# A four-stage sequence kernel on one core: the Mamba stage by channel halves, with the orders of all engines planned anew

## The reference, cut to what matters

```python
proj = h @ in_W + in_b
x1, g = (proj[..., :D], proj[..., D:])
xc = conv_general_dilated(xt, conv_w[:, None, :], padding=[(K - 1, 0)], ...)
x1 = silu(transpose(xc + conv_b[:, None]))
dbc = x1 @ dbc_W + dbc_b
delta, Bm, Cm = (dbc[..., :DTR], dbc[..., DTR:DTR + N], dbc[..., DTR + N:])
delta = softplus(delta @ dup_W + dup_b)
A_disc = exp(delta[..., None] * A)
B_x = delta[..., None] * Bm[:, :, None, :] * x1[..., None]
# scan over time: h = a * h + b
y = einsum('tbdn,btn->btd', hs, Cm)
y = silu(g) * y
```

## Time and profile before

| | us |
|---|---|
| median of 3 runs | 870.79 |
| lowest, highest | 868.19, 875.68 |
| the profiled execution | 866.0 |
| its span | 864.2 |
| TensorE busy in it | 695.4 |
| VectorE busy | 634.2 |
| ScalarE busy | 426.1 |
| GpSimd busy | 358.3 |

### The profile page before, as it was taken

One profiled execution on the slowest core, in us unless ns is written; L12 is line 12 of the kernel. 1 busy time (PEld: TensorE's weight loads), 2 busy tenths in 40 slices (PEclk: granted clock), 3 DMA queues, 4 the chain that ended last, 5 costly groups with the idle time before them and its releaser, 6 DMA issues.

```text
span 864.2 us, 12658 instructions
## 1 busy us (share of the span) xinstructions
PE 695.4 (80%) x4232; PEld 414.3 (48%) x4232; DVE 634.2 (73%) x1223; ACT 426.1 (49%) x896; POOL 358.3 (41%) x392
## 2 busy tenths in 40 slices
PE   6479648898789878988899778988798878975777
PEld 2345425445544555555545554456454554443324
DVE  1962575887889786978698687978698768846493
ACT  1325333754477255825474346825483337532542
POOL 6640331753258223942184324922293006400470
PEclk7578978998989998998999788999999698987899
DMA  5231210530145004320243014400432004100320
GB/s 131 85 127 38 82 36 10 184 129 1 38 138 174 16 1 149 131 82 0 71 152 140 0 38 135 157 27 1 135 126 98 2 16 151 47 2 6 122 75 7
DMA packets 40457, 66.11 MB, mean 77 GB/s; under 512 B 7281, under 2 KB 29634, under 8 KB 38082
## 3 DMA queue, kind: packets, MB, share of 16 engines
q1 hardware_dynamic: 38242, 64.57, 22.8%
q10 hardware_dynamic: 2176, 1.05, 0.4%
HBM read 57.68 MB, written 7.86 MB: 76 GB/s over the span
## 4 chain that ended last, share of the span: by engine, by line
PE 45%; DVE 31%; issue 11%; ACT 8%; POOL 2%; DMA 2%; SPq 1%; DVEq 0%; ACTq 0%; POOLq 0%
PE ps_s L1210 13%; PE ps_y L1210 10%; PE ps_f L1210 9%; PE ps_v L1210 8%; DVE shared L1171 5%; DVE mx L1070 4%; PE ps_n L1210 4%; DVE shared L1176 2%; DVE bn L982 1%; ACT ps_f L914 1%; ACT probs L831 1%; DVE z L1115 1%; DVE fmem L963 1%; DVE qamax L952 1%; DVE x L994 1%
## 5 line engine op out<-in xcount | busy, mean ns | idle before, releaser
L739 POOL TENSOR_TENSOR shared<-u,bcrow 128x512 f32<-128x512 f32 x128 | 205.3, 1634 | 107.7 <-DVE u L1160 84.9
L1171 DVE TENSOR_TENSOR_SCAN shared<-ps_f,shared 128x512 f32<-128x512 f32 x128 | 150.6, 1208 | 20.7 <-PE ps_y L1210 7.3
L1070 DVE TENSOR_REDUCE mx<-ps_s 128x2 f32<-128x512 f32 (+1 forms) x192 | 127.5, 687 | 48.8 <-PE ps_s L1210 47.0
L1210 PE MATMUL ps_s<-stack_mem 72*128 72x128 bf16 (+3 forms) x1024 | 149.0, 266 | 10.2 <-ACT probs L831 4.6
L1210 PE MATMUL ps_y<-shared,ident 128*128 128x512 f32 x256 | 122.3, 609 | 14.6 <-DVE shared L1176 14.6
L914 ACT ACTIVATE ps_f<-delta,amat 128x255 f32<-128x255 f32 x256 | 110.1, 476 | 32.7 <-DVE shared L1171 18.9
L1210 PEld LDWEIGHTS ps_s<-stack_mem 74*128 74x128 bf16 (+1 forms) x1024 | 87.2, 106 | 72.0 <-issue 22.2
L831 ACT ACTIVATE probs<-ps_s 128x512 f32<-128x512 f32 x192 | 106.3, 596 | 30.4 <-PE ps_s L1210 30.0
L1210 PE MATMUL ps_y<-zero_bf 128*128 128x512 bf16 x293 | 92.5, 430 | 1.4 <-DVE zero_bf L1007 1.0
L1176 DVE TENSOR_TENSOR shared<-shared,bcrow 128x1024 f32<-128x1024 f32 x64 | 91.2, 1426 | 2.2
L1210 PEld LDWEIGHTS ps_y<-shared,ident 128*128 128x128 f32 x256 | 45.7, 192 | 59.9 <-issue 36.9
(11 more groups left out here) (219 smaller groups left out, 1060.3 us busy)
## 6 DMA issues: line engine op xcount, KB each, us to landing
bcrow<-bc_dram SPq DMA_DIRECT2D x64, 512.0 KB, 4.2
stack_mem<-stack_dram SPq DMA_DIRECT2D x96, 192.0 KB
stack_dram<-parts SPq DMA_DIRECT2D x24, 256.0 KB, 2.3
x_tm<-in_L_attn_x_dram ACTq DMA_DIRECT2D x8, 128.0 KB, 2.2
xb<-in_L_attn_x_dram SPq DMA_DIRECT2D x8, 128.0 KB, 2.2
out_dram<-y_out SPq DMA_DIRECT2D x8, 128.0 KB, 2.1
fmem<-in_L_attn_conv_w_dram SPq DMA_DIRECT2D x1, 512.0 KB
lmem<-in_L_ffn_W_dram SPq DMA_DIRECT2D x2, 256.0 KB
```

The source lines that it names most:

```text
L739: G.tensor_tensor(bx[:, j % 2, c], u[:, c].unsqueeze(1).to_broadcast([P, 2, T]), bcrow[:, j % RING, 0], ALU.mult).then_inc(bx_sb, 1)
L1070: V.tensor_reduce(mx[:, a, min(i, 1), hd[0]:hd[-1] + 1:2], ps_s[:, n % 2].rearrange("p (h n) -> p h n", h=len(hd)), AX.X, ALU.max).then_in ...
L1171: V.tensor_tensor_scan(hs[:, j % HB, c].rearrange("p n t -> p (n t)"), ps_f[:, c, :], bx[:, j % 2, c].rearrange("p n t -> p (n t)"), 0.0, ...
L1210: return nc.tensor.matmul(o, lhsT, rhs, start=start, stop=stop, **kw)
```

## The change

1. The gate's product and its silu stand ahead of the convolution. The gate keeps bank 0 of ps_f; convolution half 0 goes to bank 1, half 1 to bank 0 after gsilu has read it.
2. cbias, edge and their instructions are gone. Each convolution half gets one more product: convb_row (4 rows, conv_w times in_b) with reach (4 rows of ones and zeros, row k being zero for the tokens that tap k does not reach). Setup has one VectorE product in place of five small ones, two loads in place of one, and a memset and a select more on GpSimd.
3. xc, the delta product, dpre, Abs, Exp, Ln, delta and u go by channel halves, each with its own semaphore count; GpSimd's first product of half c waits for u of half c.
4. In the last scan step the product with C and the sum into ps_y go by halves: 512 elements right behind each scan.
5. The tables of due times are new in many places: zero steps, the last FFN on TensorE, the rstd of the Mamba norm on ScalarE.

```diff
@@ SyncE, loads
-            (convw[:], conv_w.rearrange("(c p) k -> p c k", p=P)), (convb[:], conv_b.rearrange("(c p) -> p c", p=P)),
+            (convb[:], conv_b.rearrange("(c p) -> p c", p=P)),
...
+        loads.append((inb_row[:], in_b[0:DI].partition_broadcast(KC)))
+        loads.append((convb_row[:], conv_w.rearrange("d k -> k d")))
@@ ScalarE, mamba
-                act.wait_ge(edge_sb, b + 1)
-                for c in range(NC):
-                    A(xc[:, c, KC - 1:], ps_f[:, 1, c * T + KC - 1:(c + 1) * T], ACT.Silu, bias=cbias[:, 0, c:c + 1])
-                A(xc[:, :, 0:KC - 1], edge[:], ACT.Silu).then_inc(xc_sb, 1)
...
                 last.then_inc(gsilu_sb, 1)
+                for c in range(NC):
+                    yield
+                    act.wait_ge(conv_ps, b * 2 + c + 1)
+                    A(xc[:, c], ps_f[:, 1 - c, 0:T], ACT.Silu, bias=convb[:, c:c + 1]).then_inc(xc_sb, 1)
                 exp_ln_tables()
...
-                A(adisc[:, :, :, 0], zero[:], ACT.Copy)
-                chain(A(dexp, dpre, ACT.Abs))
-                chain(A(dexp, dexp, ACT.Exp, scale=-1.0))
-                A(dexp, dexp, ACT.Ln, bias=cst[:, 3:4]).then_inc(dln_sb, 1)
+                for c in range(NC):
+                    yield
+                    act.wait_ge(dl_ps, b * 2 + c + 1)
+                    A(dpre[:, c], ps_f[:, c, 0:T], ACT.Identity, bias=dupb[:, c:c + 1])
+                    chain(A(dexp[:, c], ps_f[:, c, 0:T], ACT.Abs, bias=dupb[:, c:c + 1]))
+                    chain(A(dexp[:, c], dexp[:, c], ACT.Exp, scale=-1.0))
+                    A(dexp[:, c], dexp[:, c], ACT.Ln, bias=cst[:, 3:4]).then_inc(dln_sb, 1)
+                    A(adisc[:, c, :, 0], zero[:, c], ACT.Copy)
@@ VectorE, mamba
+                for c in range(NC):
+                    yield
+                    dve.wait_ge(dln_sb, b * 2 + c + 1)
+                    V.scalar_tensor_tensor(delta[:, c], dpre[:, c], 0.0, dexp[:, c], ALU.max, ALU.add).then_inc(delta_sb, 1)
+                    dve.wait_ge(delta_sb, b * 2 + c + 1)
+                    if c == 0:
+                        dve.wait_ge(xc_sb, b * 2 + 2)
+                    V.tensor_tensor(u[:, c], delta[:, c], xc[:, c], ALU.mult).then_inc(u_sb, 1)
@@ VectorE, scan
+                        if j == N // 2 - 1:
+                            yield
+                            dve.wait_ge(hs_sb, b * 16 + 2 * j + c + 1)
+                            V.tensor_tensor(hs[:, j % HB, c], hs[:, j % HB, c], bcrow[:, j % RING, 1], ALU.mult).then_inc(hc_dve, 1)
-                    if j not in POOL_HC:
+                    if j < N // 2 - 1:
@@ TensorE, mamba
                 for c in range(NC):
-                    for k in range(KC):
-                        last = mm(ps_f[:, 1, c * T:(c + 1) * T], inWk[:, k, c * P:(c + 1) * P], hxT[:, k:k + T], start=(k == 0), stop=(k == KC - 1))
-                last.then_inc(conv_ps, 1)
-                for c in range(NC):
                     last = mm(ps_f[:, 0, c * T:(c + 1) * T], inWg[:, c * P:(c + 1) * P], hxT[:, KC - 1:])
                 last.then_inc(gate_ps, 1)
+                for c in range(NC):
+                    yield
+                    if c == 1:
+                        pe.wait_ge(gsilu_sb, b + 1)
+                    for k in range(KC):
+                        mm(ps_f[:, 1 - c, 0:T], inWk[:, k, c * P:(c + 1) * P], hxT[:, k:k + T], start=(k == 0), stop=False)
+                    mm(ps_f[:, 1 - c, 0:T], convb_row[:, c * P:(c + 1) * P], reach[:], start=False).then_inc(conv_ps, 1)
@@ PLAN, TensorE
-        "warm": [1.5, 9.5, 11, 26.6, 33.5, 39.5, 40.5, 41.5, 42.5, 53.5, 61.5, 88],
+        "warm": [13.1, 21.1, 22.7, 38.3, 38.4, 39.5, 39.7, 39.8, 40.7, 53.5, 61.5, 86.8],
```

More of the change, by code:

```diff
@@ L536, in ring_count, with hc_ready @@
             return 16 * (b * len(range(slot, N // 2, RING)) + turn + 1)
-        def hc_ready(eng, b, j):
-            on_pool = j in POOL_HC
-            mine = [i for i in range(N // 2) if (i in POOL_HC) == on_pool]
-            eng.wait_ge(hc_pool if on_pool else hc_dve, b * len(mine) + mine.index(j) + 1)
+        def hc_ready(eng, b, j, c=0):
+            eng.wait_ge(hc_dve, b * (N // 2 + 1) + j + c + 1)
         def heads(e):
@@ L652, in setup @@
                 for t_ in (xqT_mem, zero):
-                    last = G.memset(t_[:], 0.0)
-                last.then_inc(s_pool0, 1)
+                    G.memset(t_[:], 0.0)
+                chain(G.memset(reach[:], 1.0))
+                G.affine_select(out=reach[:], in_=reach[:], compare_op=ALU.is_ge, fill=0.0, base=1 - KC,
+                                pattern=[[1, T]], channel_multiplier=1).then_inc(s_pool0, 1)
                 pool.sem_inc(y_stored, 16)
@@ L1032, in setup @@
                 yield
-                chain(V.tensor_tensor(cbias[:], inb[:, 0:NC].unsqueeze(1).to_broadcast([P, KC, NC]),
-                                      convw[:].rearrange("p c k -> p k c"), ALU.mult))
-                chain(V.tensor_tensor(cbias[:, KC - 1], cbias[:, KC - 1], convb[:], ALU.add))
-                for k in reversed(range(KC - 1)):
-                    chain(V.tensor_tensor(cbias[:, k], cbias[:, k], cbias[:, k + 1], ALU.add))
+                V.tensor_tensor(convb_row[:], convb_row[:], inb_row[:], ALU.mult)
                 yield
```

136 lines of the change are left out of this document (62 added, 74 removed), and 2 rows, old and new, of the table EDGE.

## The result

The changed kernel took 880.08 us, median of 8 runs (878.27 to 880.97), the kernel before 868.36 beside it (866.50 to 875.68). Forecast were 862 and a range of 851 to 878, so the time lies above the range. In the experiments the medians are of all runs, while the ratios leave out slow runs, those more than 1.5% above the fastest of the same kernel, which moves a ratio by up to 0.006. The profiled execution took 880.24 us, its span 878.2, mean granted clock 0.868 (before 864.2 and 0.882). A granted clock of 1 is 2.4 GHz; half clock is 1.2 GHz.

What follows compares the result with a forecast made beforehand. No engine is full: each turn is a chain hopping between engines, and the clock matters as much as an edit. From 870.8, -4.4 for the edits and -4.8 for turns 4 and 6 give 862; 8-in-10 range 851 to 878.

Steps and rivals of the forecast that it cites:

- Mamba front: Gate first, convolution by halves, edge as matmul: first delta product 0.7 us later per turn, the last half 2.06 later.
- so I expect the convolution at full clock: Twelve zero products ahead of hx's transposes shorten TensorE's idle time: -0.96 in turns like 2, -0.5 on average.
- which then read like turn 2: FFN: zero pairs end the long low stretch of turns 4 and 6, 4.8 us less together.
- the scan's two gains: Per turn: 0.8 us at the scan's end by half products, 0.4 at its start by halved delta and u.
- three signs of being wrong: dbc over 1 us later; first scan no earlier than 3 us behind delta; gate to up 8 us in over two turns.
- The scan's end: Last scan pair to y: scan and half product alternate, 4.8 us instead of 5.63, a gain of 0.8 every turn.
- The prediction's 8.8 and 7.8: Its figures for convolution group start to delta product before the change, turns 2 and 4; forecast 8.6 after.
- The term of -0.4: Delta to scan on VectorE: four halves of 0.41 and two mparts start the first scan after 2.6 us, not 3.01.
- zero pair of 0.6: FFN on TensorE: two zero matmuls between gate and up product add 0.49 to 0.98 us, taken as 0.6.
- The third: Rival: the clock falls in the FFN in every turn, every turn reads like turn 4; 883 us, chance 0.17.
- two conditions: Third rival, turn's start: vals ahead ends TensorE's work earlier, and four zeros become two ahead of x3's transposes; +12.2 us.

## Why the prediction was wrong

The forecast by stretch against the two profiled executions, turns 1 to 6 together (us):

| | forecast | measured |
|---|---|---|
| gate product to VectorE's product with up | -1.2 | +4.4 |
| first projection product to the delta product | +1.2 | +8.5 |
| delta to the next y | -7.2 | -1.6 |
| y to the gate product, product with up to the projections | -1.2 | -3.2 |
| start and turn 0 | -0.5 | +1.7 |
| turn 7 | -0.3 | +1.7 |
| behind the last y | 0 | +2.4 |

So the step that failed by most is the Mamba front's "so I expect the convolution at full clock"; the FFN's "which then read like turn 2" and the scan's two gains follow. Of the prediction's three signs of being wrong two came: dbc 1.1 later than now in turn 2, the first scan 3.03 behind the delta.

**The scan's end: right, and a quarter less than forecast.** 0.44 to 0.65 a turn instead of 0.8, 0.59 in turns 2 and 3. VectorE's part is 3.8 as said; the end of TensorE's is not 1.0 behind the second half but 1.3. It isn't given back, but a lower clock hides it. From the first scan to y the kernel before takes 33.5 to 33.7 us in turns 2, 3 and 5 (clock 0.76 to 0.79 from 3 to 9 us behind delta) and 34.5 to 34.8 in turns 1, 4 and 6 (0.56 to 0.58). The changed kernel takes 33.7 to 34.0 in all six, at 0.51 to 0.58; with the end alone in halves it is 33.0 to 33.1 at 0.73 to 0.78 and 33.9 to 34.3 at 0.51 to 0.58. So the halves save some 0.5 at either level, and turns 2, 3 and 5 lost 0.6 to 0.9 to the clock.

**The Mamba front: the chain right, the clock wrong.** 2.3 us behind the last half was forecast, 2.4 came; delta product 5.6 behind which delta follows, 5.60. The group ahead of it was forecast at 6.2 and took 7.69; at full clock it takes 6.00 (turn 1), so the excess is the gate and most of half 0 at half clock, against the term "I expect the convolution at full clock". Twelve zeros did not buy that. Within the 6.00 two errors cancel: a four-row product costs 0.72 and not 0.52, and a record 0.22 at full clock and not 0.258 (20 records in 4.48 us in turn 1 before). For turn 2 the terms gave +0.7 and -0.96 for this stretch, and +1.1 came; over six turns +1.2 was forecast and +8.5 came. The prediction's 8.8 and 7.8 for the stretch before are misread: it is 9.0 (335.23 less 326.21 in the earlier trace rows) and 8.0. Its -0.96 isn't what its rows give either, 5.29 less 16 times 0.258 being 1.16.

**First products: wrong.** The term of -0.4 supposed four halves of 0.41. VectorE and GpSimd got in each other's way: the delta of half 1 took 1.08 while GpSimd's first product ran, and GpSimd's second product was late for the second scan. The halves finish the scan pair 0.5 later instead of earlier. The same shows in the old order already (a product with C took 2.18 beside GpSimd's products, 1.23 in the earlier trace rows), and the prediction used 1.23 alone. The Trainium skill (SBUF — State Buffer, section SBUF: two separate sides) has the rule: the two engines share one pair of ports under an exclusive lock; a VectorE instruction with two SBUF inputs needs it against a GpSimd one that reads SBUF, and whichever starts first holds it for its whole length. The trace agrees: delta starts behind GpSimd's product and ends 0.28 behind it, not at a shared rate. Of the 56 whole products with C in the changed kernel 15 took 2.0 to 2.3 us; all of them started behind a GpSimd product, and each ended 1.07 to 1.09 behind that product's end. In turns 2 to 5, though, doing away with the collision at delta saved at most 0.3 us a turn.

**The FFN: the zero pair of 0.6 was 0.85 in turns 1 to 5,** at half clock, and 0.62 in turn 6; the bounds of 0.49 to 0.98 held. The long stretches of turns 4 and 6 did get shorter, as the prediction said (8.75 and 8.69 became 7.23 and 6.82), but turns 2, 3 and 5 met them at 7.2 to 7.4, and turn 1 went from 6.3 to 9.6. In turns 2, 4, 5 and 6 that is at most 0.5 off the forecast; turns 1 and 3 are 2.7 and 2.0 off, since half clock took in the whole stretch of turn 1 (before, its gate product alone) and the gate product of turn 3 (before, nothing of it). The step that failed here is "which then read like turn 2", with all turns left at their old level or at turn 2's: one turn got a long stretch that had none, and turn 3 lost the full clock that it had. The two kernels with one zero table exchanged show that the table costs some 5 us; the clock of each turn under it isn't explained by these runs.

**The ends: not worked out.** The tail got no term at all, though its zero times are in the change, and cost 2.4. Turn 7 was forecast 0.3 shorter and came 1.7 longer: 2.1 stand in the eight one-row products ahead of its gate product, for which the prediction has no term either (2.07 us at half clock; every kernel here with the new times of turn 7 has 17.5 from y to the gate, every one with the old 15.4). The start was put down as hidden behind stack_mem's transfers; there SyncE spends 3.77 us at the entry behind the load by single elements, and the first maximum is 1.3 us later than in the kernel before:

```profile
17.84 3.77 SPq L559
```

That this reaches the total isn't shown.

**The rivals.** The third came nearest (883 for 880.1) and had 0.17. That is partly luck. Of its two conditions the order of vals is refuted by a run. The zeros' table does cost, but not by the missing pair ahead of x3's transposes: six zero products more there left the FFN as it was. Turns that read like turn 4, 8.7 us, did not come either (7.1 to 7.3 in turns 2 to 5, 9.5 in turn 1 alone). It gave one cause for all; the runs show several smaller ones. In ratios, with end halves as the only gain: zero table +0.7%, front +0.3%, delta in halves about +0.5% (mostly by the clock), tail +0.3% from the trace, start +0.1 to 0.2% if it counts in full, end halves -0.4%: +1.5 to +1.6% for a measured 1.2%. This is bookkeeping and no proof. Each interval is as wide as a part, the ratios come from different groups of runs, and the parts aren't independent: leaving out the two four-row products, a piece of the front, took 24 us from the changed kernel, more than the whole loss. How much of the front's and of the halves' price is clock, and why the clock falls where it does, can't be settled by these runs.

## What to carry to other kernels

Where a table of times moves instructions, cost every place in it, the last turn and the start too: here two tables of zeros, neither of which computes anything, are 1.0 of the 1.5 points in the sum above, and one turn's due times put 2.1 us of one-row products on the chain. Before two instructions are put beside each other on VectorE and GpSimd, look in the trace for the same instruction alone and in company; halving one so that the other starts earlier can lengthen it, and a shift of 0.2 us decides which of the two takes twice its time. And judge an edit that moves TensorE's idle time by the stretches that are on the chain, never by the mean clock.
